# Cross-attention block on one core: gathered q and k rows on other partitions, and another order in the setup

## The chip, the cores and the metric

The kernel runs on one core of one Trainium2 chip. The metric is the device time of one execution in microseconds, lower is better. TensorE (PE), VectorE (DVE), ScalarE (ACT) and GpSimd (POOL) each work through their own list of instructions; SyncE (SP) does little here but issue the transfers (DMAs) between HBM and the on-chip memory SBUF. The lists meet at semaphores only.

## The reference, cut to what matters

```python
B, N, C = 32, 256, 256;  M = 77;  H = 16;  D = 16;  hid = 1024
xq, c = layer_norm(x), layer_norm(context)
q = (xq @ q_w).reshape(B, N, H, D)
k, v = split((c @ kv_w).reshape(B, M, 2, H, D))
attn = einsum('bnhd,bmhd->bhnm', q, k) * D ** -0.5
attn = softmax(where(xa_mask[:, None], -finfo.max, attn), axis=-1)
x = x + einsum('bhnm,bmhd->bnhd', attn, v).reshape(B, N, C) @ proj_w + proj_b
x = x + gelu(layer_norm(x) @ fc1_w + fc1_b) @ fc2_w + fc2_b
```

## The kernel before, in words

The 32 batches are worked in 16 pairs (512 tokens, `TN`, a pair). Every engine runs `body(j, par, mlp, prep, ahead)` once a pair; bodies 0 and 1 are written out, a hardware loop runs 2 to 13, then two more are written out. Inside body j the scores, exponentials and output projection of pair j are interleaved on PE with the second MLP layer of pair j-1 and with the preparation of pair j+1: transposes of its normalised context (`cT`) and x (`xT`), `k_proj`, `q_proj`, `v_proj`, and `maxima`. Body 0 has no MLP work of an earlier pair. Where PE would stand still in the setup, `keep_warm` multiplies weights into an unused bank; nobody reads the result. Nothing but the order in which these lists are written decides what runs when.

Precise products are made of three single-pass products of high and low parts (`product`). The scores need q and k of every head side by side on the contraction rows, so q and k are stored to HBM (`qd`, `kd`: `store_q`, `store_k`) and read back as gathers of 16-row pieces into three matrices: `QR` and `KR` for a first, rough product whose row maxima (DVE, `row_max`) give the softmax shift, `QM` and `KM` for the exact scores. The contraction of `QM` is 127 rows: rows 0 to 76 hold the mask (copied by ACT or POOL from `mask_u8`, times a fixed pattern in `KM`), rows 77 to 124 hold the 16 dimensions times three terms of q, rows 125 and 126 the shift (`spread_shift`). `QR` is built alike on 125 rows, with three heads side by side on rows 77 to 124.

The setup before body 0: weights are loaded and split, pair 0 is projected, its q and k go through HBM, its twelve banks of maxima are multiplied on PE (`maxima(0, r)`) and reduced on DVE (`first_row_max`), the shifts of batch 0 and then of batch 1 are transposed (`first_shift_transpose`) and spread. Then body 0 starts with `cT(1)`, `xT(1)`, 13 `keep_warm` and `scores(0, 0)`.

Names and lines that the steps below touch, by the numbers of the profile: L1096 the rough product, L893 its reduction in the setup and L791 in the bodies, L1126 scores, L620 exp, L1200 `keep_warm`, L1042 every precise product (q, k, v, output projection `PROJ`, fc1), L1151 the transposes `hT` of the second layer norm, which wait for eight reduced banks of the next pair, L269/L270 the gather into KR, L341/L343 (L347/L349 in the setup) into QR, L276 into KM, L354/L360 into QM, L280 and L284 the stores of k and q, L294 and L288 the spread of the shift, L314 the load of `xin` (x again, for the residual), L507 POOL's `add_proj_b`, L518 POOL's `low_o`, L524 POOL's low parts of fc2's weights.

Three orders matter. POOL in body 0: `mask_rows_for_maxima(1)`, `add_proj_b(0)` (waits for `xin`), `low_o(0, 0)`, `low_o(0, 1)`. The projection of batch b waits for `low_o`, and DVE's transpose of batch 1's attention output waits for `low_o(0, 0)`, since both use the tile `oT`. SP in body 0: context and x of pair 2, store k, store half of q, gather KR, store the other half of q, gather QR (waits until q has landed in HBM), gather KM and QM.

Of the kernel before, what the change touches and what calls it, by code (L numbers as in the profile page):

```python
# [9 lines left out]
def xattn_block(nc, x, ctx, maskT, vec_columns, q_w, kv_w, proj_rows, proj_b, fc1_w, fc2_w, fc2_b, out):  # L10
# [30 lines left out]
    RROWS = QROWS + M  # L41
    RBANKS = TT * RG // 2
# [6 lines left out]
    with es:  # L49
# [28 lines left out]
        mask_u8 = sb("mask_u8", [M, NB, N], maskT.dtype)  # L78
# [32 lines left out]
        with ExitStack() as before_g:  # L111
# [4 lines left out]
            pat_m, pat_r = raw("pat_m", 1, MX), raw("pat_r", 1, MX)  # L116
# [22 lines left out]
        def max_bank(r):  # L139

            return RB[r % 4] if r < 8 else ST[r % 2]

# [92 lines left out]
        QM_LOADS, QR_LOADS, K_STORES, Q_STORES = 6 * 16, 6 * 16, 2 * 16, 4 * 16  # L235
# [26 lines left out]

        def gather_k_for_maxima(eng, j):
            if not isinstance(j, int) or j > 0:
                eng.wait_ge(k_stored, k_stores(j + 1))
            for_max = KR[M:RROWS].bitcast(F32).rearrange("p h b m -> p h (b m)")
            per_head = kd[0].rearrange("(h d) n -> d h n", d=D)
            for a in range(3):
                eng.dma_start(for_max[a * D:(a + 1) * D, a:H - 1:3], per_head[:, a:H - 1:3]).then_inc(qr_loaded, 16)  # L269
            eng.dma_start(for_max[2 * D:, H - 1:H], per_head[:, H - 1:H]).then_inc(qr_loaded, 16)  # L270
# [29 lines left out]
        def _(sp):  # L300
# [38 lines left out]
            def gather_q_for_maxima(j):  # L339
                sp.wait_ge(q_stored, q_stores(j + 1))  # L340
                sp.dma_start(QR[M:RROWS, 0:RG - 1].bitcast(F32),  # L341
                             qd[0, 0:(RG - 1) * QROWS].rearrange("(g r) n -> r g n", r=QROWS)).then_inc(qr_loaded, 16)
                sp.dma_start(QR[M:RROWS, RG - 1].bitcast(F32), qd[0, H * D - QROWS:]).then_inc(qr_loaded, 16)  # L343

            def first_q_for_maxima(b, done):
                toks = slice(b * N, (b + 1) * N)
                sp.dma_start(QR[M:RROWS, 0:RG - 1, toks].bitcast(F32),  # L347
                             qd[0, 0:(RG - 1) * QROWS, toks].rearrange("(g r) n -> r g n", r=QROWS)).then_inc(done, 16)
                sp.dma_start(QR[M:RROWS, RG - 1, toks].bitcast(F32), qd[0, H * D - QROWS:, toks]).then_inc(done, 16)  # L349

            def first_q_for_scores(b, rows, done):
                toks = slice(b * N, (b + 1) * N)
                for a in rows:
                    sp.dma_start(QM[M + a:SHIFT:3, :, toks].bitcast(F32),  # L354
                                 qd[(0, 1, 0)[a], :, toks].rearrange("(h d) n -> d h n", d=D)).then_inc(done, 16)

            def gather_q_for_scores(j):
                sp.wait_ge(s_mm, PB * j)
                for a, part in enumerate((0, 1, 0)):
                    sp.dma_start(QM[M + a:SHIFT:3].bitcast(F32),  # L360
                                 qd[part].rearrange("(h d) n -> d h n", d=D)).then_inc(qm_loaded, 16)
# [27 lines left out]
            sp.wait_ge(first_q_stored, G * 16)  # L389
            first_q_for_maxima(0, qr_loaded)  # L390
            first_q_for_maxima(1, qr_late)
            sp.wait_ge(pat_done, 2)
            gather_k_for_scores(sp, 0, (0, 1))
            first_q_for_scores(0, (0, 2), qm_loaded)
# [4 lines left out]
            spread_first_shift(sp, 0)  # L399
            first_q_for_scores(1, (0, 1, 2), qm_late)  # L400
            spread_first_shift(sp, 1)
            load_mask(1)
            load_xin(0, 0)

            def body(j, par, mlp, prep, ahead):
# [3 lines left out]
                if prep:  # L409
                    store_k(j + 1)  # L410
# [25 lines left out]
        def _(pool):  # L436
# [4 lines left out]
            pool.memset(pat_m[:], 0.0).then_inc(patterns, 1)  # L441
            pool.memset(pat_r[:], 0.0).then_inc(patterns, 1)
# [3 lines left out]
            pool.wait_ge(patterns, 2)  # L446
# [965 lines left out]
```

## Time and profile before

| | us |
|---|---|
| median of 3 runs | 783.61 (782.18 to 784.01) |
| the profiled execution, device time | 780.9 |
| its span in the trace | 779.0 |
| its mean granted TensorE clock | 0.993 |

The page gives busy times of the engines, the span in 40 slices, the chain of waits that ended last and the costliest groups of instructions. A wait is listed with the engine that stood still, the line of its next instruction and what released it. A gap on PE before body 1 is worth reading, since the later bodies repeat.

### The profile page before, as it was taken

The page shows a single profiled execution, that of the slowest core. Times are in us where ns is not written, and L with a number is a line of the kernel's source. Part 1 is how long each engine was busy: PE and PEld are TensorE (multiplying, and loading weights), DVE is VectorE, ACT ScalarE, POOL GpSimd, SP SyncE. Part 2 cuts the span into 40 slices and gives each one's busy share as a digit, 9 for nine tenths or more (in the row PEclk, how much of TensorE's full clock was granted, in tenths as well). Part 3 has the DMA queues.
Part 4 walks back from the last instruction along what each step waited for, and adds up shares of the span by engine and source line. Part 5 has one row for each costly group of instructions (what it writes and reads, how often), then busy time and mean ns, then how long its engine had stood idle before and what let it go on. Part 6 is the DMA issues. An engine that isn't in the chain of part 4 may idle for free.

```text
span 779.0 us, 17095 instructions
## 1 busy us (share of the span) xinstructions
PE 755.7 (97%) x5647; PEld 636.6 (82%) x5647; DVE 600.8 (77%) x1376; ACT 525.2 (67%) x776; POOL 225.4 (29%) x217
## 2 busy tenths in 40 slices
PE   8796999999999999999999999999999999999998
PEld 7665788797988879798887979888797988879687
DVE  6777778788887888788787888878787888867453
ACT  5755776767677676767767676776767677676732
POOL 3153240423324042332404233240423324041230
PEclk9899999999999999999999999999999999999999
DMA  7999486694948759494875949487594948649100
GB/s 254 173 170 135 93 157 110 156 125 124 140 114 160 113 151 127 130 135 109 161 113 151 127 132 135 107 161 113 152 127 133 137 104 162 112 115 130 32 28 28
DMA packets 90869, 99.93 MB, mean 128 GB/s; under 512 B 8854, under 2 KB 66166, under 8 KB 90838
## 3 DMA queue, kind: packets, MB, share of 16 engines
q1 hardware_dynamic: 90134, 98.83, 68.0%
q10 hardware_dynamic: 704, 0.69, 0.3%
q8 instruction: 18, 0.29, 0.2%
q14 instruction: 13, 0.11, 0.1%
HBM read 68.18 MB, written 30.28 MB: 126 GB/s over the span
## 4 chain that ended last, share of the span: by engine, by line
PE 81%; DMA 7%; DVE 3%; ACT 3%; issue 3%; SPq 1%; ACTq 0%; POOL 0%; DVEq 0%; POOLq 0%
PE A L1042 25%; PE F L1042 14%; PE ST L1126 8%; PE A L1135 7%; PE F L1180 7%; PE F L1181 6%; PE F L1182 6%; PE ST L1096 3%; DMA QR<-qd 3%; PE A L1151 2%; PE A L1096 1%; DMA kd<-k_lo 1%; ACT probs L620 1%; ACT L714 1%; DMA qd<-q_lo 1%
## 5 line engine op out<-in xcount | busy, mean ns | idle before, releaser
L620 ACT ACTIVATE probs<-ST 78x512 f32<-78x512 f32 x256 | 137.5, 587 | 51.0 <-PE ST L1126 46.8
L1180 PE MATMUL F<-w_hi,g_hi 128*128 128x256 f32 x480 | 138.4, 288 | 0.0
L1181 PE MATMUL F<-w_lo,g_hi 128*128 128x256 f32 x480 | 134.3, 280 | 0.0
L1182 PE MATMUL F<-w_hi,g_lo 128*128 128x256 f32 x480 | 134.2, 280 | 0.0
L720 DVE TENSOR_TENSOR g_lo<-g_f,g_hi 128x512 fp32r<-128x512 f32 x128 | 88.2, 689 | 33.2 <-ACT g_hi L654 30.7
L640 ACT ACTIVATE QM<-mask_u 77x2048 fp32r<-77x2048 uint8 x60 | 111.2, 1901 | 0.0
L1126 PE MATMUL ST<-QM,KM 127*78 127x256 f32 x512 | 94.6, 296 | 4.5 <-ACT probs L620 2.2
L1180 PEld LDWEIGHTS F<-w_hi,g_hi 128*128 128x128 f32 x480 | 90.4, 188 | 6.2 <-issue 6.2
L1126 PEld LDWEIGHTS ST<-QM,KM 127*78 127x78 f32 x512 | 59.0, 146 | 39.0 <-ACT probs L620 30.6
L1181 PEld LDWEIGHTS F<-w_lo,g_hi 128*128 128x128 f32 x480 | 90.7, 189 | 0.0
L1182 PEld LDWEIGHTS F<-w_hi,g_lo 128*128 128x128 f32 x480 | 90.2, 188 | 0.0
L501 POOL TENSOR_TENSOR pool_carrier<-eps 128x1 f32<-128x1 f32 x15 | 2.9, 193 | 274.0 <-DVE g_hi L851 269.1
L518 POOL TENSOR_TENSOR oT_lo<-g_f,oT_hi 128x512 fp32r<-128x512 f32 x32 | 41.6, 1299 | 138.3 <-ACT oT_hi L627 138.3
L645 ACT ACTIVATE xT_hi<-A 128x512 fp32r<-128x512 f32 x32 | 17.4, 595 | 88.8 <-PE A L1151 88.8
L791 DVE TENSOR_REDUCE shift<-ST 128x6 f32<-128x462 f32 (+1 forms) x120 | 63.3, 569 | 16.8 <-PE ST L1096 15.4
L1135 PE MATMUL A<-probs,V 78*32 78x256 f32 x1024 | 68.7, 385 | 0.4 <-ACT probs L620 0.4
L652 ACT ACTIVATE g_f<-F,bias 128x512 f32<-128x512 f32 x64 | 44.1, 689 | 34.0 <-issue 20.1
L808 DVE STREAM_TRANSPOSE o_tok<-A 128x512 f32<-128x512 f32 x64 | 43.1, 693 | 20.3 <-PE A L1135 20.3
L652 ACT ACTIVATE g_f<-A,bias 128x512 f32<-128x512 f32 x64 | 44.1, 689 | 19.6 <-PE A L1042 14.3
L1042 PE MATMUL F<-xT_hi,w_hi 128*128 128x512 f32 x128 | 52.5, 410 | 0.3 <-DVE xT_lo L720 0.3
L1042 PE MATMUL A<-xT_hi,w_hi 128*128 128x512 f32 x128 | 51.8, 405 | 0.0
L720 DVE TENSOR_TENSOR xT_lo<-A,xT_hi 128x512 fp32r<-128x512 f32 x64 | 42.7, 688 | 11.7 <-ACT xT_hi L645 10.7
(188 smaller groups left out, 1916.0 us busy)
## 6 DMA issues: line engine op xcount, KB each, us to landing
QM<-qd SPq DMA_DIRECT2D x45, 512.0 KB, 14.9
xa<-in_x SPq DMA_DIRECT2D x16, 512.0 KB, 4.0
qd<-q_hi SPq DMA_DIRECT2D x32, 256.0 KB, 2.1
xin<-in_x SPq DMA_DIRECT2D x16, 512.0 KB, 5.6
qd<-q_lo SPq DMA_DIRECT2D x30, 256.0 KB, 2.0
out<-xin SPq DMA_DIRECT2D x30, 256.0 KB, 7.6
KM<-kd SPq DMA_DIRECT2D x48, 156.0 KB, 6.9
QR<-qd SPq DMA_DIRECT2D x15, 480.0 KB, 5.4
```

The source lines that it names most:

```text
L620: act.activation(probs[:, quad % NSLOT, 2 * (p % 2):2 * (p % 2) + 2], ST[p % 2][0:MX].rearrange("p (h n) -> p h n", n=N), ACT.Exp, scale=S ...
L640: act.activation(QM[0:M, heads], mask_u8[:].rearrange("p b n -> p (b n)").unsqueeze(1).to_broadcast([M, H // MASK_PARTS, TN]), ACT.Copy).t ...
L652: act.activation(g_f[k % 2][:], FC1[k % 4][:], ACT.Gelu, bias=b1).then_inc(gelu_done, 1)
L720: return dve.tensor_tensor(dst, src, hi.bitcast(F32), ALU.subtract)
L791: dve.tensor_reduce(shift[:, 6 * c:6 * c + n, t], max_bank(r)[:, 0:n * MX].rearrange("p (h m) -> p h m", m=MX)[:, :, 0:M], X, ALU.max).the ...
L808: dve.transpose(o_tok[:, qq].rearrange("p n e -> p (n e)"), A[2 * b + qq][:]).then_inc(o_tok_done, 1)
L1042: last = pe.matmul(dst, a, b, start=(n == 0), stop=(n == 3 * len(terms) - 1))
L1126: last = pe.matmul(ST[p % 2][0:MX, i * N:(i + 1) * N], KM[:, h, b], QM[:, h, b * N:(b + 1) * N], start=True, stop=True)
L1135: last = pe.matmul(A[2 * b + qq][32 * i:32 * (i + 1), g * N:(g + 1) * N], V[:, b, 4 * q + i], probs[:, quad % NSLOT, i], start=True, stop= ...
L1180: pe.matmul(dst, g_hi[:, k, tok], w2_hi[:, k], start=(k == 0), stop=False)
L1181: pe.matmul(dst, g_hi[:, k, tok], w2_lo[:, k], start=False, stop=False)
L1182: last = pe.matmul(dst, g_lo[:, k, tok], w2_hi[:, k], start=False, stop=(k == HC - 1))
```

## The change

1. **Rows.** The three terms of head dimension d now stand on rows 7d, 7d+1, 7d+2 (`term_rows`, step 7) and the 77 keys' mask on the rows between and behind them, in `QM`, `KM`, `QR` and `KR`. The mask is laid out on 125 rows ahead of the launch, with zeros on the rows of the terms, and copied whole; so the gathers of q must now wait for the mask copy (`mask_max`, `mask_qk`). The gathers into KR and QR are three DMAs each, of 16 rows (before: four for KR; for QR two, of 48 rows). The gather into QM is cut in two halves of the heads, six DMAs, each half behind two of ACT's four mask copies. The pattern is one tile, `pat`, with seven instructions of POOL that select instead of four.
2. **Setup, PE.** `first_maxima` takes the place of `maxima(0, r)` with more PSUM banks (`FIRST_RB`). `cT(1)` and `xT(1)` run behind the eighth of the twelve banks; banks 10 and 11 run behind `scores(0, 1)`. The 13 `keep_warm` ahead of the scores and 8 others are gone. In body 0 `k_proj(1)` runs ahead of `scores(0, 2)`, `q_proj(1, 0)` ahead of `scores(0, 4)` and `q_proj(1, 1)` ahead of the first `attend`.
3. **Setup, DVE and ACT.** `normalise_x(1)` runs ahead of the second half of the reductions; the MLP's weight parts are spread between k_low and q_low of pair 1. ACT makes `QM`'s mask of batch 0 in gaps of the first 16 us, and k_high and q_high of pair 1 behind the exponentials 1, 3 and 5 (before: 3, 5 and 9).
4. **Loads.** `load_xin(0)` moves from the end of the setup to behind the gather of QR(1) in body 0.

On PE, from the eighth bank on to the second pair of scores (`A<-pw_hi`, the projection, comes later); before:

```order
L1096 MATMUL A<-KR,QR 128x234 x2
L1205 MATMUL A<-ident,shift 64x128
L1200 MATMUL A<-kvw_hi 128x512
L1096 MATMUL ST<-KR,QR 128x234
...
L1205 MATMUL A<-ident,shift 64x128
L1200 MATMUL A<-kvw_hi 128x512 x4
L1050 MATMUL A<-ident,cn 128x77 x4
L1056 MATMUL A<-ident,xa 128x128 x8
L1200 MATMUL F<-kvw_hi 128x512 x13
L1126 MATMUL ST<-QM,KM 78x256 x8
```

and after:

```order
L1252 MATMUL F<-KR,QR 128x234 x2
L1258 MATMUL A<-ident,shift 64x128
L1083 MATMUL A<-ident,cn 128x77 x4
L1089 MATMUL A<-ident,xa 128x128 x8
L1252 MATMUL F<-KR,QR 128x234
...
L1157 MATMUL ST<-QM,KM 78x256 x4
L1252 MATMUL F<-KR,QR 128x234 x3
L1252 MATMUL F<-KR,QR 128x78
L1258 MATMUL A<-ident,shift 64x128
L1075 MATMUL A<-cT_hi,kvw_hi 128x156
```

The transposes of pair 1 moved ahead of the last four banks, the weight multiplications between them left, and the products of k (`A<-cT_hi,kvw_hi`) start behind four of the score products, where eight stood before.

On SP, from the last spread of the setup on into body 0; before:

```order
L294 DMA QM<-o_tok 2x16x128 x2
L327 DMA mask_u<-in_mask_BxSxS_bk 77x2x256
L314 DMA xin<-in_x 128x4x256
L320 DMA cn<-in_ctx 77x2x256
L308 DMA xa<-in_x 128x4x256
L280 DMA kd<-k_hi 128x2x156
...
L284 DMA qd<-q_lo 128x512
L341 DMA QR<-qd 48x5x512
L343 DMA QR<-qd 48x512
L276 DMA KM<-kd 16x16x156 x3
L360 DMA QM<-qd 16x16x512 x3
L327 DMA mask_u<-in_mask_BxSxS_bk 77x2x256
```

and after:

```order
L305 DMA QM<-o_tok 2x16x128
L338 DMA mask_u<-in_mask_BxSxS_bk 125x2x256
L331 DMA cn<-in_ctx 77x2x256
L319 DMA xa<-in_x 128x4x256
...
L295 DMA qd<-q_lo 128x512
L355 DMA QR<-qd 16x6x512
L355 DMA QR<-qd 16x5x512 x2
L325 DMA xin<-in_x 128x4x256
L287 DMA KM<-kd 16x16x156
```

The load of xin now stands behind two stores' round trips and the gather into QR.

The core of the diff:

```diff
+        FIRST_RB = (ST[0], ST[1], A[0], A[3], ST[0], ST[1], A[0], F[1], F[0], A[0], F[1], F[0])
+        def term_rows(a):
+            return slice(a, a + STEP * (D - 1) + 1, STEP)
-                eng.dma_start(KM[M + a:SHIFT:3].bitcast(F32).rearrange("p h b m -> p h (b m)"),
+                eng.dma_start(KM[term_rows(a)].bitcast(F32).rearrange("p h b m -> p h (b m)"),
...
             def gather_q_for_maxima(j):
                 sp.wait_ge(q_stored, q_stores(j + 1))
-                sp.dma_start(QR[M:RROWS, 0:RG - 1].bitcast(F32),
-                             qd[0, 0:(RG - 1) * QROWS].rearrange("(g r) n -> r g n", r=QROWS)).then_inc(qr_loaded, 16)
-                sp.dma_start(QR[M:RROWS, RG - 1].bitcast(F32), qd[0, H * D - QROWS:]).then_inc(qr_loaded, 16)
+                sp.wait_ge(mask_max, j + 1)
+                per_head = qd[0].rearrange("(h d) n -> d h n", d=D)
+                for a in range(3):
+                    sp.dma_start(QR[term_rows(a), 0:(H - a + 2) // 3].bitcast(F32), per_head[:, a:H:3]).then_inc(qr_loaded, 16)
...
-            def gather_q_for_scores(j):
-                sp.wait_ge(s_mm, PB * j)
+            def gather_q_for_scores(j, half):
+                sp.wait_ge(mask_qk, MASK_PARTS * j + (half + 1) * MASK_PARTS // 2)
+                heads = slice(half * H // 2, (half + 1) * H // 2)
...
@@ sync, end of the setup and body @@
             load_mask(1)
-            load_xin(0, 0)
...
                     gather_q_for_maxima(j + 1)
+                    if not mlp:
+                        load_xin(0, 0)
                     gather_k_for_scores(sp, j + 1)
-                    gather_q_for_scores(j + 1)
+                    gather_q_for_scores(j + 1, 0)
                 if mlp:
                     store(j - 1, 1 - par, 0)
+                if prep:
+                    gather_q_for_scores(j + 1, 1)
@@ vector, end of the setup @@
             normalise_ctx(1)
+            normalise_x(1)
             for r in range(RBANKS // 2, RBANKS):
                 first_row_max(r)
             first_shifts(1)
-            normalise_x(1)
-            mlp_weight_low(0)
-            mlp_weight_low(1)
@@ tensor, setup and body @@
+            for r in range(8):
+                first_maxima(r)
+                if 4 <= r < 7:
                     keep_warm(A[2], 1)
-            first_shift_transpose(1)
-            keep_warm(A[2], 4)
+            first_shift_transpose(0)
+            cT(1)
+            pe.wait_ge(first_shiftT_done, 1)
+            xT(1, 1)
+            xT(1, 0)
+            first_maxima(8)
+            first_maxima(9)
...
-                if not mlp:
-                    keep_warm(F[0], 13)
...
+                if not mlp:
+                    first_maxima(10)
+                    first_maxima(11)
+                    first_shift_transpose(1)
+                    k_proj(j + 1)
                 scores(j, 2)
```

## Rows read from the trace of the kernel before

**Rows 1.** The page: busy times, PE and granted clock in 40 slices.
```profile
PE 755.7 (97%) x5647; PEld 636.6 (82%) x5647; DVE 600.8 (77%) x1376; ACT 525.2 (67%) x776; POOL 225.4 (29%) x217
PE   8796999999999999999999999999999999999998
PEclk9899999999999999999999999999999999999999
```

**Rows 2.** Busy time by stretch: stretch, its length, PE, PEld, DVE, ACT, POOL, clock, DMA share, GB/s.
```profile
20.00:40.00 20.00, 15.65 (x100) 13.71 (x99) 14.95 (x42) 13.39 (x20) 3.04 (x3) 0.83 1.03 167
60.00:80.00 20.00, 14.03 (x85) 12.54 (x86) 14.54 (x35) 11.46 (x12) 5.93 (x8) 0.91 1.06 131
400.00:500.00 100.00, 99.64 (x739) 84.06 (x738) 81.47 (x186) 71.60 (x108) 27.03 (x24) 1.00 0.68 127
```

**Rows 3.** PE's waits: who was waited for, us in total, times, longest.
```profile
PE ST L1096 <- DMA QR<-qd: 6.4, 4, 2.9
```

**Rows 4.** PE in order of time: start, us, instruction, idle before it and its releaser.
```profile
29.06 1.20 PE L1096 MATMUL ST<-KR,QR 125*128 125x234 f32 x4 [2.91 <-DMA QR<-qd]
39.77 3.26 PE L1200 MATMUL F<-kvw_hi 128*128 128x512 f32 x13
61.77 0.36 PE L1042 MATMUL A<-pw_hi,oT_hi 128*128 128x256 f32 x1 [1.94 <-POOL oT_lo L518]
65.93 0.72 PE L1096 MATMUL ST<-KR,QR 125*128 125x234 f32 x4 [2.49 <-DMA QR<-qd]
74.66 1.09 PE L1151 MATMUL A<-ident,o_tok 128*128 128x128 f32 x8 [1.71 <-DVE shift L791]
111.54 0.71 PE L1096 MATMUL ST<-KR,QR 125*128 125x234 f32 x4 [0.54 <-DMA QR<-qd]
```

**Rows 5.** Stretches as in rows 2: gathers alone, stores, idle and half-speed PE.
```profile
28.00:42.00 14.00, 11.51 (x59) 9.73 (x60) 11.88 (x28) 6.70 (x11) 3.12 (x2) 0.82 1.18 128
57.00:59.00 2.00, 1.88 (x14) 1.23 (x15) 1.90 (x5) 0.07 (x1) 0.00 (x0) 1.00 0.77 273
59.80:66.00 6.20, 1.77 (x14) 1.57 (x13) 4.71 (x11) 5.27 (x5) 3.48 (x4) 1.00 0.93 137
67.60:71.10 3.50, 3.50 (x16) 3.16 (x16) 2.52 (x10) 1.44 (x1) 0.49 (x2) 0.55 1.09 133
```

**Rows 6.** DMAs issued at 29.36, 24.52, 48.05, 57.26 and 84.44: KB, us to landing.
```profile
QM<-qd SPq DMA_DIRECT2D x1, 256.0 KB, 12.1
QR<-qd SPq DMA_DIRECT2D x1, 48.0 KB, 4.5
kd<-k_lo SPq DMA_DIRECT2D x1, 156.0 KB, 7.0
qd<-q_lo SPq DMA_DIRECT2D x1, 256.0 KB, 2.3
xin<-in_x SPq DMA_DIRECT2D x1, 512.0 KB, 5.5
```

**Rows 7.** SP's spread of the first shift, and ACT's mask copies, in order of time.
```profile
34.04 1.42 SPq L294 DMA_DIRECT2D QM<-o_tok  x2
...
24.42 3.88 ACT L579 ACTIVATE QM<-mask_u 77x1024 fp32r<-77x1024 uint8 x4
```

**Rows 8.** DVE in order of time.
```profile
40.04 0.48 DVE L754 TENSOR_REDUCE A<-A 128x4 f32<-128x308 f32 x1
44.11 1.45 DVE L866 SCALAR_TENSOR_TENSOR w_lo<-raw_w,columns,w_hi 128x512 fp32r<-128x512 f32 x1
46.93 0.66 DVE L770 SCALAR_TENSOR_TENSOR k_lo<-A,bias,k_hi 128x154 fp32r<-128x154 f32 x2 [1.37 <-ACT k_hi L603]
68.62 0.69 DVE L826 TENSOR_TENSOR xin<-A,xin 128x512 f32<-128x512 f32 x1 [0.91 <-PE A L1042]
```

**Rows 9.** POOL in order of time.
```profile
52.71 2.37 POOL L507 TENSOR_TENSOR xin<-xin,projb 128x1024 f32<-128x1024 f32 x1
60.35 1.27 POOL L518 TENSOR_TENSOR oT_lo<-g_f,oT_hi 128x512 fp32r<-128x512 f32 x1 [5.27 <-ACT oT_hi L627]
```

More of the change, by code:

```diff
@@ L688, in body @@
                     exp(j, p)
[L689 removed]
+                    if not mlp and p == 1:
+                        first_shift_rows(1)
                         k_high(j + 1)
[L691 removed]
+                    if mlp and prep and p == 3:
+                        k_high(j + 1)
+                    if not mlp and p == 3:
                         q_high(j + 1, 0)
[L693 removed]
+                    if mlp and prep and p == 5:
+                        q_high(j + 1, 0)
+                    if not mlp and p == 5:
+                        q_high(j + 1, 1)
+                    if mlp and prep and p == 9:
                         q_high(j + 1, 1)
@@ L980, in body @@
                     ln_moments(j + 2)
-                if prep:
+                if mlp and prep:
                     q_low(j + 1, 1)
@@ L1200, in keep_warm, with first_maxima @@
                     pe.matmul(bank[:], kvw_hi[:, 0, 0:P], kvw_hi[:, 0], start=True, stop=True)
+            def first_maxima(r):
+                t, c = divmod(r, RG // 2)
+                tok = slice(t * P, (t + 1) * P)
+                if r == 0:
+                    pe.wait_ge(qr_loaded, QR_LOADS)
+                    pe.wait_ge(mask_max, 1)
+                if r == RBANKS // 2:
+                    pe.wait_ge(qr_late, 3 * 16)
+                if r in (4, 5, 6):
+                    pe.wait_ge(max_done, r - 3)
+                if r == 7:
+                    pe.wait_ge(q_lo_done, G)
+                if r == 8:
+                    pe.wait_ge(setup_done, QKV_READY + 1)
+                if r > 8:
+                    pe.wait_ge(max_done, r - 2)
+                for half in range(2):
+                    h = 6 * c + 3 * half
+                    n = min(3, H - h)
+                    last = pe.matmul(FIRST_RB[r][:, 3 * half * MX:(3 * half + n) * MX].rearrange("p (h m) -> p h m", m=MX),
+                                     QR[:, 2 * c + half, tok], KR[:, h:h + n, t // TB], start=True, stop=True)
+                last.then_inc(r_mm, 1)
             def first_shift_transpose(b):
                 pe.wait_ge((first_shift_done, shift_done)[b], 2)
-                pe.wait_ge(first_shiftT_done, b)
-                pe.transpose(SHT[0:2 * H * TB, b * P:(b + 1) * P], first_shift[:, b].rearrange("p t h -> p (t h)"),
+                pe.transpose(FIRST_SHT[b][0:2 * H * TB, 0:P], first_shift[:, b].rearrange("p t h -> p (t h)"),
                              ident[:]).then_inc((first_shiftT_mm, shiftT_mm)[b], 1)
@@ L1255, in body @@
                 pe.wait_ge(v_done, j + 1)
-                if prep:
+                if mlp and prep:
                     cT(j + 1)
@@ L1286, in body @@
                 scores(j, 7)
-                if prep:
+                if mlp and prep:
                     q_proj(j + 1, 1)
@@ L1395 @@
         'ctx_1024': _np.asarray(inputs['ctx_1024']),
-        'mask_BxSxS2_bk0': _np.asarray(inputs['mask_BxSxS2_bk0']).transpose(0, 2, 1),
+        'mask_BxSxS2_bk0': None,
         'vectors': _np.concatenate([_np.asarray(inputs[n]) for n in _VECTORS]).reshape(-1, 128).T,
     }
+    m = _np.asarray(inputs['mask_BxSxS2_bk0'])
+    key = _np.arange(m.shape[2])
+    rows = _np.where(key < 64, 7 * (key // 4) + 3 + key % 4, key + 48)
+    laid_out['mask_BxSxS2_bk0'] = _np.zeros((m.shape[0], 125, m.shape[1]), m.dtype)
+    laid_out['mask_BxSxS2_bk0'][:, rows] = m.transpose(0, 2, 1)
     for name in _PLAIN:
```

119 lines of the change are left out of this document (65 added, 54 removed).

## The prediction

> **What bounds the kernel now.** I read the 40 slices and the windows first. From the fifth slice on PE is busy nine tenths or more of every slice at the full clock [rows 1], and a stretch in the loop shows 99.64 of 100 us [rows 2]. The reader is to see there that no other engine and no transfer can give anything in the loop, unless PE waits for it. The setup and body 0 are different: 4.35 us of 20 to 40 and 5.97 us of 60 to 80 have no PE work [rows 2]. Then PE's waits: the longest are for the gather into QR, four times, 6.4 us [rows 3]. In order of time they are 2.91 us ahead of the first maxima, 2.49 us ahead of pair 1's, and 0.54 us in body 1; the remaining one is 0.46 us (what is left of the 6.4) in a later body [rows 3, 4]. What looks busy is partly filler: the 13 keep_warm of 3.26 us ahead of the first scores do nothing but pass time [rows 4]. So the span is a chain of setup up to the transposes hT of pair 0, which start at 74.66 [rows 4], and behind it a fixed amount of PE work. I forecast when hT starts after the change, and what the loop gives.
>
> **The loop, part by part.** PE has the same products there. The gathers show 128 GB/s at a DMA share of 1.18, where stores from all partitions show 273 GB/s at 0.77 [rows 5]: the DMA engines are occupied and move little, so something at the gathers' rows holds them up. Those rows are 77 to 124, and the change spreads them over nearly the whole height. I take 1.8 times the rate, between 1 (the rows are not the reason) and 2.1 (273 against 128).
>
> The Trainium skill (SBUF — State Buffer, "Door 1: The DMA port swizzle") says that a transfer's rate follows how many of 16 ports its partitions reach, and that partitions 64 to 127 reach eight of them. By it each old gather reaches eight ports and each new one 14, a rate of 1.75 times; its own 27 GB/s a port would allow 218 GB/s before, and the trace shows 128, so the page's limit is not reached here and the ratio is not certain.
>
> Two waits of together 0.9 to 1.0 us (body 1 and one later body) are what a faster QR gather can take off the loop. The third issue of the QR gather costs 0.45 us of SP, and the rate more than repays it. Gain 0.9; with an unchanged rate a loss of up to 0.5 in each of the 15 gathers, 6 us, less where there is slack. The QM gather now starts behind ACT's mask copies, some 5 to 8 us later; its scores come more than 20 us behind it, so that cover is wide. SP's store of the first half of the output and the next mask load, which stand behind it in SP's list, move by 3 us at most and are waited for 15 us later. Nothing.
>
> **The setup, step by step.** Times are those of the trace before, and in brackets what the step had there.
>
> 1. ACT's two mask copies of 0.97 us each [rows 7] before the weights arrive are free (ACT stands still there); one more of 0.97 us sits ahead of the copy of x's transpose, of which about 0.5 is covered by ACT's idle time. q is 0.3 us later. POOL's three more selections of 0.25 us end before anybody needs its next result.
> 2. First maxima: three issues of 0.45 us instead of two; the second landed 4.5 us after its issue [rows 6]. With the faster rate I take 2.8 us behind the third: 24.5 + 0.9 + 2.8 = 28.2 (29.06, rows 4). Bounds 27.5 to 30.
> 3. Banks 0 to 7 and the first shift transpose: 4.95 us at half clock, as before; ACT's copy 0.3; two spread issues of 0.7 each [rows 7], of which the second lands some 2.2 us after its start (between 2.0, the fastest small transfers of the trace, and 3): 28.2 + 4.95 + 0.3 + 0.75 + 2.2 = 36.4. PE meanwhile does cT(1), xT(1) and banks 8 and 9, which are ready at about 36. The gather into QM was the real limit before: the last of it was issued at 29.36 and landed 12.1 us later, at 41.5 [rows 6]. At 1.8 times the rate it lands near 35. So the first scores start at 36.6 (43.02, behind the 13 keep_warm).
> 4. Banks 10 and 11 behind them, DVE's two reductions and the shifts: +2.3, to 38.9. Then DVE splits cT and xT of pair 1, 4.07 us as from 40.04 to 44.11 [rows 8], one weight part of 0.7 and k_low 0.6: k_lo is ready at 44.3 (47.55). The old weight part took 1.45 us [rows 8], while POOL was on its own weight parts; POOL now has them behind it.
> 5. Store of k: the second DMA took 7.0 us [rows 6] because x, xin and QM were in flight; now they aren't, and I take 2.6 as in later bodies: 44.3 + 0.4 + 2.6 = 47.3 (55.0).
> 6. KR gather 1.3, q stores 0.9 of issue, of which the last lands after 2.3 [rows 6]: 51.4 (59.6), and 1.25 for QR's three issues: 52.6. **QR lands near 55.5 and is no longer waited for.**
> 7. What is late next: the load of xin. It had its place at 40.07 and a lot of slack; now it is issued at 52.6. Alone it took 5.5 us [rows 6]; I take 4.6, since no other writer competes but QR. It lands at 57.2, POOL adds the bias in 2.37 and makes low_o in 1.27 [rows 9]: 60.9. **The projection of batch 0 starts at 60.9 (61.77, rows 4).** PE's eight keep_warm end at 57.1, so PE stands still for 3.8 us.
> 8. Batch 1: DVE's transpose 0.7, ACT's copy 0.6, POOL's low_o 1.3: 63.6 for the projection. At full clock it is over at 65.1, DVE is free from 65.4, and adds the projection of batch 1 to x at 65.4 (68.62, rows 8). From there to hT DVE is busy without a gap for 6.0 us in both. Gain 3.2.
>
> **The clock.** The trace shows PE at a granted clock of 1.00 while it does 1.77 us in 6.2, and then 0.55, near the lower of its two levels (1.2 against 2.4 GHz), over 3.5 us of full work [rows 5]. PE's pause of step 7 is as long as those. At half speed the two projections and the maxima between them (3.6 us) last up to 3.6 us more, of which the first projection's and half of the second's are on the path: I take 1.5, between 0 and 2. The sparse work between 33 and 42 costs something too, but DVE's splits run beside it: 0.3, between 0 and 1.3.
>
> Sum: 3.2 - 1.5 - 0.3 + 0.9 = 2.3 us. 780.9 - 2.3 = 778.6 as a profiled execution. The median of the runs shown is 2.7 us above the profiled one; I keep that distance: 783.6 - 2.3 = **781.3**.
>
> **Rivals.**
> - *The load of xin doesn't bind, or binds less.* If it lands with QR, 1 to 2 us earlier, and the clock stays up, projections start at 59.5 and the gain is 3.2 + 1.4 + 0.9 = 5.5: 778.1. For it: POOL waits for nothing else, and the unforced chain (q stored at 51.4) would allow 56. Against it: two round trips through HBM stand ahead of the load in SP's list, and each of my terms for them is already near the shortest of the trace.
> - *Moved slack eats the gain.* Half clock from 37 to 44 makes the products of k and q 1.3 to 1.4 us longer each, q_lo is ready at 50.5 instead of 48, and xin, two round trips later, pushes the projections to 63.5: gain 3.2 - 2.6 - 1.5 + 0.9 = 0, 783.6.
> - *Slower.* The rows are not what holds the gathers up, and they stay at 128 GB/s. Then QM of batch 0 lands at 42, the first scores start there, banks 10 and 11, the splits and k_lo follow at 49.7, and xin is issued at 58 and lands at 63; the projection starts at 66.7 against 61.77. That is 5 us more, partly won back since the waits on DVE shrink by 2.2, and the QR waits in the loop stay or grow: 787.5. It decides once the gathers' rate is under about 1.2 times the old one. For it: packets that were written to neighbouring rows might wait for something other than the row, such as the read side, which doesn't change. Against it: the same buffers in HBM are written, and x is read, at twice the rate.
>
> **How the numbers follow.** Forecast, xin as the new limit with gain 1.2 to 3.6: 0.47. Less bound: 0.20. Gain eaten: 0.23. Slower: 0.10. A measurement of this kernel tells 0.3%, 2.35 us, from no change. The forecast's own range (780.0 to 782.4) lies across that bound, half on each side, so faster takes 0.24 + 0.20 and some of the rest: 0.46, same 0.44, slower 0.10. The range for 8 in 10 takes in the first two rivals and their spread: 778.0 to 784.6. It leaves out the slow gathers, and a gain above 5.6.
>
> **What the profile after would show.** Step 2: QM and QR gathers well above 128 GB/s at a share under 1.1. Step 3: no wait of the first scores behind 38. Steps 5 and 6: QR's wait of 2.49 us gone and those of the loop too. Step 7: POOL's L507 group waits for the DMA of xin, and a wait of PE for POOL's oT_lo of 3 to 5 us instead of 1.94. Clock: a half-speed stretch that begins between 58 and 64. I'm wrong if the DMA rate in the gathers is as before, if PE waits in the loop for the mask or QM, or if PE's wait for oT_lo is released by ACT's copy rather than by the bias on POOL.

## The result: slower, where faster or no change was forecast

| | before | after |
|---|---|---|
| median of 6 runs, us | 783.56 (782.18 to 784.01) | 786.9 (784.94 to 789.42) |
| ratio to before, 95% interval | | 1.006 (1.0037 to 1.0084) |
| the profiled execution, device time | 780.9 | 784.94 |
| its span / its mean granted clock | 779.0 / 0.993 | 783.2 / 0.983 |

The time lies above the range on record (778.0 to 784.6) and on the other side of no change. The page of after, for [rows 1]:

```profile
PE   8886999999999999999999999999999999999998
...
PEclk9888999999999999999999999999999999999999
```

From the fifth slice on PE and its clock read as before. The changed kernel's stretches, for [rows 2] and [rows 5], with the columns of [rows 2]:

```profile
20.00:40.00 20.00, 17.43 (x104) 15.10 (x102) 14.28 (x42) 12.07 (x19) 5.76 (x6) 0.83 0.78 215
42.00:46.00 4.00, 3.32 (x16) 3.32 (x17) 3.83 (x7) 0.43 (x2) 0.00 (x0) 0.50 0.23 62
60.00:80.00 20.00, 12.34 (x62) 10.53 (x61) 10.70 (x28) 7.40 (x6) 8.22 (x9) 0.79 0.53 137
400.00:500.00 100.00, 99.61 (x736) 84.05 (x735) 81.77 (x188) 70.97 (x107) 27.04 (x24) 1.00 0.41 121
```

The loop moves the same data at a DMA share of 0.41 instead of 0.68, and PE is as full as before. The loss lies at 60 to 80: 12.34 us of PE work instead of 14.03, at a granted clock of 0.79 instead of 0.91. PE in order of time, for [rows 4]:

```profile
29.47 1.20 PE L1252 MATMUL ST<-KR,QR 125*128 125x234 f32 x4
38.81 0.67 PE L1157 MATMUL ST<-QM,KM 127*78 127x256 f32 x4 [1.47 <-DMA QM<-o_tok]
41.26 0.42 PE L1258 MATMUL A<-ident,shift 128*64 128x128 f32 x1 [1.40 <-DVE shift L934]
42.68 0.50 PE L1075 MATMUL A<-cT_hi,kvw_hi 128*128 128x156 f32 x1 [1.00 <-DVE cT_lo L751]
...
66.70 0.55 PE L1075 MATMUL A<-pw_hi,oT_hi 128*128 128x256 f32 x1 [5.19 <-POOL oT_lo L541]
78.58 1.97 PE L1182 MATMUL A<-ident,o_tok 128*128 128x128 f32 x8 [1.85 <-DVE shift L822]
```

Three things are to be seen. The first scores start at 38.81, where they started at 42.86 in the kernel before, right behind the 13 keep_warm of [rows 4]. Twenty-eight microseconds later that lead of 4 us is a lag of 4.9: the projection of batch 0 starts at 66.70 instead of 61.77, behind a wait of 5.19 us for POOL's `oT_lo`. And the transposes hT start 3.92 us later (78.58 against 74.66) and take 1.97 us, against 1.09. The span is 4.2 us longer: 3.9 from hT's start, 0.9 from hT's own half-speed start, and -0.6 from everything behind it, in which two waits for QR of together 1.0 us are gone and a little more half-speed work has come.

What released POOL is in its own list, and what released that, in SP's. POOL's and then SP's rows of after, in order of time:

```profile
46.36 2.75 POOL L525 CAST QR<-mask_u 125x3072 fp32r<-125x3072 uint8 x1
62.99 2.34 POOL L530 TENSOR_TENSOR xin<-xin,projb 128x1024 f32<-128x1024 f32 x1 [13.88 <-DMA xin<-in_x]
65.29 1.26 POOL L541 TENSOR_TENSOR oT_lo<-g_f,oT_hi 128x512 fp32r<-128x512 f32 x1
```

```profile
44.40 0.40 SPq L319 DMA_DIRECT2D xa<-in_x  x1
...
47.46 0.47 SPq L291 DMA_DIRECT2D kd<-k_lo  x1
...
51.71 1.91 SPq L280 DMA_DIRECT2D KR<-kd  x3
...
54.28 0.43 SPq L295 DMA_DIRECT2D qd<-q_lo  x1
56.65 1.85 SPq L355 DMA_DIRECT2D QR<-qd  x3
58.55 0.59 SPq L325 DMA_DIRECT2D xin<-in_x  x1
```

POOL stands still for 13.88 us for the load of `xin`. SP issues that load at 58.55, since the gather into KR waits until k has landed in HBM (51.7) and the gather into QR until q has (56.6). The last rows of after are the DMAs: KB and us from issue to landing. The first three are medians of the whole run (in before, the same gather into KM took 6.9 us and the store of the output 7.6), the next two are of 42 to 64 us.

```profile
QM<-qd SPq DMA_DIRECT2D x96, 256.0 KB, 4.0
KM<-kd SPq DMA_DIRECT2D x48, 156.0 KB, 3.0
out<-xin SPq DMA_DIRECT2D x30, 256.0 KB, 3.1
...
kd<-k_lo SPq DMA_DIRECT2D x1, 156.0 KB, 4.2
xin<-in_x SPq DMA_DIRECT2D x1, 512.0 KB, 4.4
```

The share of the queue that carries them fell from 68.0 to 42.4% at 98 MB in both:

```profile
q1 hardware_dynamic: 90134, 98.83, 68.0%
```

```profile
q1 hardware_dynamic: 91766, 98.18, 42.4%
```

(before first, after second). So the rows did what was claimed for them: the share fell by a factor of 1.6 (the forecast took 1.8 for the rate), and the landing times by more. The rest of the change ate it.

### The profile page after: what moved, and what is told of

Read it like the earlier page. It is cut to its first block, busy times and chain, and to the rows that moved or that the text cites. A ratio compares the mean times of both kernels' runs of the same rounds, so it can differ in the third digit from the quotient of the medians.

```text
span 783.2 us, 17155 instructions
## 1 busy us (share of the span) xinstructions
PE 758.2 (97%) x5626; PEld 639.1 (82%) x5626; DVE 602.0 (77%) x1376; ACT 526.0 (67%) x776; POOL 225.4 (29%) x219
## 3 DMA queue, kind: packets, MB, share of 16 engines
q1 hardware_dynamic: 91766, 98.18, 42.4%
## 4 chain that ended last, share of the span: by engine, by line
PE 87%; issue 5%; ACT 3%; DMA 2%; DVE 2%; POOL 1%; SPq 0%; ACTq 0%; DVEq 0%; POOLq 0%
PE A L1075 26%; PE F L1075 14%; PE ST L1157 9%; PE A L1166 8%; PE F L1211 7%; PE F L1212 6%; PE F L1213 6%; PE ST L1127 3%; PE A L1182 2%; PE A L1127 1%; ACT L745 1%; ACT probs L643 1%; DMA raw_q<-in_L_xattn_q_w 1%; PE F L1220 0%; PE A L1264 0%
## 5 line engine op out<-in xcount | busy, mean ns | idle before, releaser
L663 ACT ACTIVATE QM<-mask_u 125x2048 fp32r<-125x2048 uint8 x60 | 111.3, 1902 | 0.0
L822 DVE TENSOR_REDUCE shift<-ST 128x6 f32<-128x462 f32 (+1 forms) x120 | 63.4, 571 | 16.1 <-PE ST L1127 14.9
L530 POOL TENSOR_TENSOR xin<-xin,projb 128x1024 f32<-128x1024 f32 x16 | 38.1, 2380 | 60.4 <-DVE g_lo L751 46.6
```

Of the source, the lines that this page charges most:

```text
L663: act.activation(QM[0:RROWS, heads], mask_u8[:].rearrange("p b n -> p (b n)").unsqueeze(1).to_broadcast([RROWS, H // MASK_PARTS, TN]), ACT ...
L822: dve.tensor_reduce(shift[:, 6 * c:6 * c + n, t], max_bank(r)[:, 0:n * MX].rearrange("p (h m) -> p h m", m=MX)[:, :, 0:M], X, ALU.max).the ...
```

## Experiments

The kernel before ran beside every group of kernels; its medians there were 782.1, 782.8 and 782.2 us. Three theories had to be told apart:

- **X**: the load of `xin` in its new place costs what was lost. Its rival: the new order or the rows do, and `xin` only shows the wait.
- **M**: the mask is now loaded with 125 rows, and this holds up the loads of the weights behind it. Its rival: the spread of `raw_q`'s landing is chance.
- **O**: the new order of the setup is worth its 4 us of earlier scores. Its rival: the 13 keep_warm were time that the chain behind needs anyway.

### X taken out and put in alone

The changed kernel with `xin` loaded where it was before (a_xin_early), and the kernel before with `xin` moved (b_xin_late). Line numbers are left out.

```diff
             load_mask(1)
+            load_xin(0, 0)
...
-                    if not mlp:
-                        load_xin(0, 0)
                     gather_k_for_scores(sp, j + 1)
```

> The changed kernel with one thing undone: the load of xin(0) stands at the end of the setup again, behind the mask load. Theory X (the late load of xin is the new bound): POOL no longer waits 13.88 us for it, low_o of batch 0 follows ACT's copy at about 59.3 instead of 65.3, the projection starts near 60.6 instead of 66.7, hT near 72 instead of 78.6, and the median falls by 6 to 7 us, to 780 to 781. Theory C (PE's sparse work lets the clock fall, and that is the loss): PE's pause before the projection shrinks but the half-speed stretches from 39 to 46 stay; at most 2 us, 785. Theory F (the first 20 us got slower): no change, 787.

> The kernel before with one thing changed: the load of xin(0) behind the gather of QR(1) in body 0. Theory X: it is issued at about 60.4 and lands at 65 to 66 (QR and KM are in flight), POOL's bias and low_o take 3.6 us, the projection starts near 69.5 instead of 61.8, and the time grows by 6 to 8 us, to 790 to 791. Theories C and F: the late load is hidden and the time stays within 2 us of 783.6.

Measured: a_xin_early 779.2 us, ratio 0.9963 (0.9943 to 0.9983), a little below what theory X expected; b_xin_late 789.28 us, ratio 1.0074 (1.0047 to 1.0101), a little below too. POOL and PE in a_xin_early, then in b_xin_late:

```profile
49.01 2.83 POOL L529 TENSOR_TENSOR xin<-xin,projb 128x1024 f32<-128x1024 f32 x1
...
60.07 1.31 POOL L540 TENSOR_TENSOR oT_lo<-g_f,oT_hi 128x512 fp32r<-128x512 f32 x1 [8.23 <-ACT oT_hi L649]
```

```profile
61.53 0.36 PE L1074 MATMUL A<-pw_hi,oT_hi 128*128 128x256 f32 x1 [0.26 <-POOL oT_lo L540]
```

```profile
66.95 2.34 POOL L508 TENSOR_TENSOR xin<-xin,projb 128x1024 f32<-128x1024 f32 x1 [13.10 <-DMA xin<-in_x]
```

```profile
70.65 0.55 PE L1043 MATMUL A<-pw_hi,oT_hi 128*128 128x256 f32 x1 [9.69 <-POOL oT_lo L519]
```

With the load in its old place the bias is added at 49.01, as a job of POOL's idle time, and PE waits 0.26 us instead of 5.19. The same edit costs 5.8 us in the kernel before (0.0074 of 782.1) and 7.6 in the changed one (1.006 less 0.9963, of 782). X is shown from both sides.

### The rows alone, and the mask on 128 rows

rows_only is the kernel before with part 1 of the change (the diff ahead of the prediction, from `term_rows` to the gathers) and nothing else. rows_mask128 is the same with the mask laid out and loaded on 128 rows, of which 125 are used; a_mask128 is the changed kernel with that one edit.

```diff
-        mask_u8 = sb("mask_u8", [RROWS, NB, N], maskT.dtype)
+        mask_u8 = sb("mask_u8", [P, NB, N], maskT.dtype)
...
-    laid_out['mask_BxSxS2_bk0'] = _np.zeros((m.shape[0], 125, m.shape[1]), m.dtype)
+    laid_out['mask_BxSxS2_bk0'] = _np.zeros((m.shape[0], 128, m.shape[1]), m.dtype)
```

> The kernel before with the new rows (gathers, mask on 125 rows, pattern, the waits that they need) and nothing of the new order; xin is loaded early as before. If the rows make the gathers faster and that is all: maxima of pair 1 wait 2 us less at 65.9, the QR waits in the loop go (1 us), the 13 keep_warm still stand ahead of the first scores: 1 to 4 us faster, 780 to 782.5. Theory F (the front is slower because of the mask's 125 rows): the weights for q land 1.2 us later as in the changed kernel, and the first gather into QR starts near 25.5 instead of 24.2: the gain shrinks to 0 to 2 us.

> The kernel before with the new rows alone (as rows_only), and the mask laid out on 128 rows instead of 125, which changes nothing but its load. Theory M (a load of 125 rows is carried by few DMA engines and holds up the weights queued behind it): the weights for q land at 8.6 to 8.9 instead of 9.9 to 10.2, the first banks of maxima start 1.3 us earlier, and the median falls by about 1.3 us against rows_only, to a ratio near 0.991 of the kernel before. Theory N (the late weights come from more bytes, 62.5 against 38.5 KB, or by chance): 64 KB land as late, no change against 0.993.

> The changed kernel with the mask laid out on 128 rows. Theory M: the weights for q land at 8.7 instead of 9.95, everything up to the load of xin moves 1.3 us forward, and the median falls by 1.3 to 2 us: ratio 1.002 to 1.003 against 1.004 to 1.008. Theory N: no change, 1.005.

Measured: rows_only 777.89, ratio 0.9928 (0.9905 to 0.9951), faster than both ranges expected of it; rows_mask128 776.7, 0.9914 (0.9893 to 0.9935); a_mask128 784.03, 1.0009 (0.999 to 1.0028), against 1.006 without the edit.

When PE gets `raw_q`, in before, after, rows_only and a_mask128, in this order:

```profile
8.85 1.02 PE L1189 MATMUL ST<-columns,raw_q 128*128 128x1 f32 x8 [1.00 <-DMA raw_q<-in_L_xattn_q_w]
```

```profile
10.09 1.02 PE L1220 MATMUL ST<-columns,raw_q 128*128 128x1 f32 x8 [1.91 <-DMA raw_q<-in_L_xattn_q_w]
```

```profile
10.18 1.02 PE L1208 MATMUL ST<-columns,raw_q 128*128 128x1 f32 x8 [2.84 <-DMA raw_q<-in_L_xattn_q_w]
```

```profile
8.76 1.02 PE L1220 MATMUL ST<-columns,raw_q 128*128 128x1 f32 x8 [0.60 <-DMA raw_q<-in_L_xattn_q_w]
```

In the five profiles with the mask on 125 rows (after, rows_only, a_xin_early, a_warm28, a_dve) it is 9.6 to 10.2; in the others, where the mask has 77 or 128 rows, 8.6 to 9.1. This much of M is shown: about 1.1 us in the mean. The bytes are not the reason, since 128 rows are more of them. A rule bears on it: the Trainium skill (DMA: Bandwidth & Descriptors, "Why a DMA increments its semaphore by 16 and not by 1") says that such a transfer is spread over the largest number of DMA engines up to 16 that divides the slowest dimension of both its sides. By it 125 rows go to 5 engines, 128 to all 16 and 77 to 11. The traces agree in direction; no row here shows which engine carried what.

The late weight may have a sequel. Of the stretch from 12 to 18 us, before, after and rows_only in this order:

```profile
12.00:18.00 6.00, 5.58 (x36) 4.89 (x35) 5.96 (x11) 3.39 (x7) 0.00 (x0) 1.00 0.78 250
```

```profile
12.00:18.00 6.00, 6.00 (x31) 5.28 (x31) 4.61 (x12) 4.76 (x7) 0.00 (x0) 0.72 0.36 111
```

```profile
12.00:18.00 6.00, 6.00 (x22) 5.07 (x23) 2.98 (x8) 2.34 (x4) 0.00 (x0) 0.50 0.36 111
```

After PE has waited 1.9 or 2.8 us for the weight, it works the transposes and the projection of pair 0 at a granted clock of 0.72 and 0.50, near the lower level (1.2 GHz); after 1.0 us (before), at 1.00. In rows_only the first maxima come at 32.86 instead of 29.06, and still the kernel is faster than before. The length of that wait does not decide it, though: a_dve waited 1.42 us there and was granted 1.00, a_warm28 waited 1.10 and was granted 0.50, and best1, with 128 rows and no such wait, 0.84. What decides the clock there stays open. So does the size of M. In the changed kernel the edit took the ratio from 1.006 to 1.0009, some 4 us, but its one profile, of one of the longest of its runs (786.65), shows no gain (784.8 of span against 783.2: the first maxima come at 28.11, and the projection, which waits for `xin`, at 67.24). In the kernel with the rows alone it took 0.0014, within the intervals, and with `xin` early it shows nothing either: 0.9963 in a_xin_early, 0.9955 in best1 below, which has this edit and another.

### The clock, by more keep_warm

a_warm28 is the changed kernel with 28 `keep_warm` in PE's pause ahead of the projection of batch 0, where the changed kernel and the kernel before have 8.

```diff
-                    keep_warm(F[0], 8)
+                    keep_warm(F[0], 28)
```

> The changed kernel with 28 instead of 8 keep_warm in PE's pause before the projection of batch 0 (20 more are about 4.7 us at full clock, inside the wait of 5.2 us). Theory C: the clock stays at 1.00 from 62 on, the projections, the transposes hT and v_proj run at full speed, and 2 to 3.5 us are won, 783.5 to 785. Theory X alone: the projection still starts at 66.7, DVE's reductions set hT, and only what ran at half clock behind hT (1.4 us) comes back: 785.5.

Measured: 785.52, ratio 1.0032 (1.0014 to 1.005). PE, and the stretch from 60 to 80 us, which had a clock of 0.79 in after:

```profile
70.74 0.36 PE L1075 MATMUL A<-pw_hi,oT_hi 128*128 128x256 f32 x1 [0.36 <-POOL oT_lo L541]
...
81.53 1.09 PE L1182 MATMUL A<-ident,o_tok 128*128 128x128 f32 x8 [1.85 <-DVE shift L822]
```

```profile
60.00:80.00 20.00, 17.53 (x116) 12.73 (x114) 12.56 (x31) 10.61 (x11) 8.30 (x9) 1.00 0.49 139
```

With the pause filled, the clock stays at 1.00, and from the start of the projection to the end of hT it takes 11.9 us, where after took 13.9 (66.70 to 80.55). That is the low end of what theory C expected. The span of this execution doesn't show it (784.7 against 783.2), because its front, which the edit doesn't touch, was late: the first maxima come at 32.70, with the clock at 0.50 from 12 to 18. The medians differ by as much, but the intervals of 1.0032 and 1.006 meet. So the clock's part is seen in one profile each, and its size in the median, some 2 us, isn't settled.

### DVE's weight parts

The forecast had 0.7 us for the weight part ahead of k_low, which took 0.74, and no term for the one between k_low and q_low. That one took 2.80 in after, beside POOL's mask cast of 2.75 (above, at 46.36). DVE of after, in order of time:

```profile
46.27 0.66 DVE L801 SCALAR_TENSOR_TENSOR k_lo<-A,bias,k_hi 128x154 fp32r<-128x154 f32 x2 [0.34 <-ACT k_hi L626]
46.85 2.80 DVE L897 SCALAR_TENSOR_TENSOR w_lo<-raw_w,columns,w_hi 128x512 fp32r<-128x512 f32 x1
...
50.24 0.74 DVE L897 SCALAR_TENSOR_TENSOR w_lo<-raw_w,columns,w_hi 128x512 fp32r<-128x512 f32 x1
```

The same instruction took 0.74 three microseconds later. The part that waits ends just behind POOL's cast (at 49.65; the cast at 49.11). The Trainium skill (SBUF — State Buffer, "Who interferes with whom") says that a VectorE instruction with two inputs in SBUF contends with a GpSimd instruction that reads SBUF, and that this is an exclusive lock; the rows agree. The two k_low, which ran while the cast had begun and read a bank of PSUM, weren't held up (0.66 for both). a_dve moves two parts behind q_low:

```diff
-                    if not mlp:
-                        mlp_weight_low(1)
                     q_low(j + 1, 0)
                 if not mlp:
-                    mlp_weight_low(2)
                     q_low(j + 1, 1)
+                    mlp_weight_low(1)
+                    mlp_weight_low(2)
                     mlp_weight_low(3)
```

> The changed kernel with DVE's weight parts 1 and 2 of the MLP behind both low parts of q in body 0. Theory P (DVE's weight part with two inputs in SBUF stands still while POOL copies the mask, 2.80 us against 0.74): the low part of q's first half starts near 47.5 instead of 49.6, the gather into KR, both stores and the load of xin come 1.5 to 2 us earlier, and the median falls by as much: ratio about 1.003. The weight part is then free to be long where nobody waits. Rival: q_high on ACT (48.4 to 49.1) and q_proj on PE set q's low part, so at most 0.5 us is won.

Measured: 786.16, ratio 1.0045 (1.0028 to 1.0062), no different from the changed kernel. Its DVE:

```profile
48.68 0.75 DVE L807 SCALAR_TENSOR_TENSOR q_lo<-A,bias,q_hi 128x512 fp32r<-128x512 f32 x1 [2.47 <-ACT q_hi L632]
```

DVE now waits 2.47 us for ACT's q_high, which itself waits 1.49 us for PE's products of q. And SP's next step, the gather into KR, waits for k's store to land (51.7 in after), not for q_lo. The 2.80 were real, large, and off the path.

### The order alone

order_only is the changed kernel without part 1 and with `xin` in its old place: parts 2 and 3 on the old rows. At the gathers:

```diff
-                eng.dma_start(KM[term_rows(a)].bitcast(F32).rearrange("p h b m -> p h (b m)"),
+                eng.dma_start(KM[M + a:SHIFT:3].bitcast(F32).rearrange("p h b m -> p h (b m)"),
```

> The kernel before with the new order of PE, DVE and ACT in the setup and body 0, the rows as before, xin loaded early. If the gathers at 128 GB/s set the first scores, as I read the trace of before: they start near 41.5 to 43 as before, k and q of pair 1 follow DVE's splits behind them, k_lo is ready near 49 instead of 47.6, and the time is 0 to 3 us above the kernel before (783 to 786). If the order is good by itself: 780 or less.

Measured: 785.56, ratio 1.0036 (1.0018 to 1.0053). PE of order_only:

```profile
42.24 1.11 PE L1139 MATMUL ST<-QM,KM 127*78 127x256 f32 x4 [5.50 <-DMA QM<-o_tok]
```

With the old rows the scores wait 5.50 us for DMAs: the six gathers into QM ahead of them land after 8.7 us in the median, and the 13 `keep_warm` had lain in that wait. The order needs the rows; the next group asks whether it is worth anything with them.

### All mended, in both orders

best1 is the changed kernel with three edits shown above: `xin` early, the mask on 128 rows, the weight parts behind q_low. best1_warm has 28 keep_warm besides, in the place of a_warm28's, ahead of the projection of batch 0. (What was expected of it speaks of a place ahead of the first maxima; no run changed the `keep_warm` there, so its question on the first 20 us was not put.) rows_mask128_5 is rows_mask128 once more.

> The changed kernel with its three faults mended together: xin loaded at the end of the setup again, the mask on 128 rows, and the MLP's weight parts 1 and 2 behind q_low(1, 1) on DVE. Theory (the faults cost 7 us, 1.2 us and about 0.5 us, and are independent; the new order of the setup then gives nothing over the old one): hT of pair 0 starts at 71 to 72.5, the time is 776 to 778, a ratio to the kernel before of 0.991 to 0.995, no better than the rows alone with the mask on 128 rows (776.7 of 782.8, 0.991). Rival (the new order is worth its 4 us of earlier scores once nothing behind it waits): hT at 69 or earlier, 772 to 774, a ratio of 0.986 to 0.989.

> The same three mended, with 28 products of keep_warm ahead of the first maxima where the changed kernel has 8 (the kernel before has 28). If the half clock of the first 20 us is what the new order pays with, the first maxima and scores run at the full clock and hT starts 1 us sooner: a ratio 0.001 to 0.003 under that of the version with 8. If the products only occupy PE where a transpose or a weight is waiting for it, they push the first maxima from 28.5 to over 31, as they did at 32.7 with the 125-row mask, and nothing is won: a ratio equal or 0.001 to 0.003 above.

> The old order with the new rows and the mask on 128 rows, the fastest so far, once more beside the two versions in the new order, in five rounds, so that the order can be compared on one chip. A repeat should give 0.991 of the kernel before, within 0.002. If the new order with its faults mended is worth something, that version stands at least 0.002 below this one; if not, within 0.002 or above.

Measured: best1 779.93, ratio 0.9955 (0.9933 to 0.9977); best1_warm 783.75, 1.0008 (0.999 to 1.0025); rows_mask128_5 775.55, 0.991 (0.988 to 0.9941). The fastest kernel of the study is the old order with the new rows, twice: 0.9914 and 0.991. Both kernels with the new order are slower than it, and best1 misses the range I had given it. The intervals of 0.9955 and 0.991 just overlap, but ten of best1's twelve runs took longer than five of the other's six. The same comparison with the mask on 125 rows, a_xin_early against rows_only, gives 0.9963 and 0.9928. PE and the stretch from 40 to 50 us, of rows_mask128_5 and then of best1:

```profile
41.88 0.64 PE L1145 MATMUL ST<-QM,KM 127*78 127x256 f32 x4
42.97 0.94 PE L1145 MATMUL ST<-QM,KM 127*78 127x256 f32 x4 [0.45 <-ACT probs L639]
...
69.55 1.09 PE L1170 MATMUL A<-ident,o_tok 128*128 128x128 f32 x8 [1.84 <-DVE shift L810]
```

```profile
40.00:50.00 10.00, 9.53 (x66) 7.18 (x66) 8.52 (x15) 5.55 (x11) 9.35 (x7) 1.00 0.89 240
```

```profile
38.78 0.67 PE L1155 MATMUL ST<-QM,KM 127*78 127x256 f32 x4 [1.25 <-DMA QM<-o_tok]
...
41.23 0.42 PE L1256 MATMUL A<-ident,shift 128*64 128x128 f32 x1 [1.40 <-DVE shift L933]
42.65 0.50 PE L1073 MATMUL A<-cT_hi,kvw_hi 128*128 128x156 f32 x1 [1.00 <-DVE cT_lo L750]
...
45.29 1.06 PE L1155 MATMUL ST<-QM,KM 127*78 127x256 f32 x4
...
73.01 1.97 PE L1180 MATMUL A<-ident,o_tok 128*128 128x128 f32 x8 [1.85 <-DVE shift L821]
```

```profile
40.00:50.00 10.00, 7.77 (x32) 6.78 (x33) 7.03 (x15) 3.62 (x9) 5.47 (x4) 0.66 0.63 182
```

Here is where the lead goes. The new order starts the scores 3.1 us earlier, by leaving out 3.26 us of `keep_warm`. But PE waits 1.25 us ahead of them, for the shift of batch 0, and 1.40 and 1.00 us behind them, for DVE, which has the shift of batch 1 and the splits of pair 1 to do: 3.65 us, about the same time in another place. And only the first four score products have the lead. The next four stand behind these waits and behind the products of k, and start at 45.29 where the old order starts them at 42.97; ACT has no scores to work on meanwhile (it waits 3.58 us there). The projection of batch 0 then starts at 61.74, against 58.68 in the old order. After these waits PE's clock is 0.50 (42 to 46 us in after, above, and in best1), while in the old order it stays at 1.00, and the products of k, 0.28 us each there, take 0.42. The chain that counts, k into HBM, gains nothing: k_lo starts at 46.24 in best1 and at 45.96 in rows_mask128_5.

The granted clock also goes with how the runs of one kernel spread. Of the runs that were timed, each with its own mean granted clock:

| kernel | lowest and highest time, us, with its clock | runs |
|---|---|---|
| before (beside the last group) | 779.78 at 0.995; 787.59 at 0.987 | 23 |
| rows_mask128_5 | 773.52 at 0.996; 779.13 at 0.987 | 6 |
| best1 | 774.78 at 0.993; 782.35 at 0.982 | 12 |
| best1_warm | 781.39 at 0.987; 785.92 at 0.984 | 12 |
| after | 784.94 at 0.983; 789.42 at 0.976 | 6 |

The one run of best1 at 0.993 is as fast as the rows alone at 0.996 and 0.991 (774.5 and 776.1), and at 0.987 three runs of best1 took 778.6 to 780.1 beside 779.1. At an equal clock the two orders are worth about the same, and the new one is granted the lower clock in most of its executions. That is what the records show together; it doesn't say what is cause and what is effect, since a pause of PE costs time and can cost clock at once. No run filled the pauses between 38 and 43 us. a_warm28 filled a pause of 5.2 us further on, and that kept the clock up there. best1_warm put the same products where best1 has no pause: the projection moves from 61.74 to 66.06, hT from 73.01 to 76.61, and the ratio from 0.9955 to 1.0008. How best to fill those gaps stays open.

## Why the prediction was wrong, step by step

The bound was forecast rightly: `xin` is what binds, POOL waits for it, PE waits for `oT_lo` (forecast 3 to 5 us, 5.19 measured), a half-speed stretch begins there, and the waits for QR are gone. What failed is the path up to the issue of `xin`, steps 2 to 7: every term of it was too short, 6.0 us together. The largest miss is step 5, the store of k, where the lag grows by 1.8 us; next is the setup up to the first maxima, 1.3 us. So the term "Gain 3.2" of the sum was a loss of 3.8 (add_x of batch 1 at 72.41 instead of 68.62). With it fell the idea that earlier scores make everything behind them earlier: k_lo was to be ready at 44.3 and was ready at 46.9, where the rows in the old order have it at 46.6. The forecast said: projection at 60.9. It is at 66.70, and the terms add up like this:

| step | forecast | measured | lag so far |
|---|---|---|---|
| 2, first maxima | 28.2 | 29.47 | 1.3 |
| 3, first scores | 36.6 | 38.81 | 2.2 |
| 4, k_lo ready | 44.3 | 46.9 | 2.6 |
| 5, k in HBM | 47.3 | 51.7 | 4.4 |
| 6, q in HBM | 51.4 | 56.6 | 5.2 |
| 7, xin issued | 52.6 | 58.55 | 6.0 |
| 7, xin landed | 57.2 | 63.0 | 5.8 |
| 7, projection of batch 0 | 60.9 | 66.70 | 5.8 |
| 8, add_x of batch 1 | 65.4 | 72.41 | 7.0 |

- **Steps 1 and 2.** I counted ACT's copies of the mask and not its load, though the diff showed it (77 rows became 125). It stands ahead of the weights: 1.2 us. The gather into QR was issued at 25.88 (forecast 24.5), and PE, which had worked at a clock of 0.72 from 12 to 18, was busy up to 29.47 and waited for no gather.
- **Step 3.** The wait that ends last was the spread of the shift, as the forecast had it (36.4, and QM before it). The step was 0.9 us too short.
- **Step 5 failed most.** "Because x, xin and QM were in flight; now they aren't": x still was. SP issues `xa` of pair 2 at 44.40, 512 KB that take 4.1 us, right ahead of the store of k, which took 4.2 instead of 2.6. I had moved `xin` out of the queue in my head, and x with it. That x alone makes the difference isn't shown: in rows_mask128_5 x was in flight as long behind the issue of k_lo (to 48.2, the issue at 47.12), and that store took 3.1.
- **Step 6.** Issues of the gathers. I took some 0.42 us each, as for the gathers of before; the new ones take 0.62 to 0.64 (1.85 for three into QR, 1.91 for three into KR). 1.2 us on the path.
- **Step 7.** The load itself took 4.4 (4.6 forecast), and POOL 2.34 and 1.26: right. The issue was late by all that stood ahead of it.
- **Step 8 and the clock.** 1.5 was taken for the two projections at half speed. The path lost 1.2 there (lag from 5.8 to 7.0), and 0.9 more in hT, for which there was no term; a_warm28, at a clock of 1.00, is 2.0 us shorter over the same work.
- **The loop.** 0.9 forecast, 1.0 of QR waits gone. Right. Its rate was taken as 1.8 times, and the share fell by 1.6 times. The count of eight ports for "each old gather" passed over those into KR, which wrote 16 neighbouring rows each; they are small, and landed after 2.0 us before and 2.2 after.
- **The rival "gathers stay slow"** was the only one that I let end on the slower side, with 0.10, and it did not happen. That the projection came at 66.7, to the tenth the time written down for that rival, is chance: it came there by the forecast's own road, with longer terms. The rival "moved slack eats the gain" had its direction, and 63.5 as its worst. The forecast said of its terms that each was "already near the shortest of the trace", as an argument against the earlier rival; the same words are a warning that the sum of a chain of such terms comes out too short, and the range made no room for that. The distance from 60.9 to no change (61.77) was less than 1 us, while `xin` in its old place had 6.8 us of slack: it landed at 51.2 and was needed at 58.0, which is 60.35 less 2.37. The row of its load in the kernel before, issued at 40.07:

```profile
xin<-in_x SPq DMA_DIRECT2D x1, 512.0 KB, 11.1
```

The 5.5 us of [rows 6], from which the forecast took its "alone", are those of a load issued at 358.10; the one at 84.44 took 5.9.

And what the sum left out:

- **What was missed as a gain.** The rows are worth 0.7 to 0.9% (6 to 7 us) by themselves, where the loop's 0.9 and step 2 to 3 were all that I could name. Nearly all of it is the setup: in rows_mask128_5 the wait for QR of 2.49 us is gone, k and q of pair 1 are in HBM 4 to 5 us earlier (50.2 and 55.3, by the issue of the gathers that wait for them; 55.0 and 59.6 before), and hT starts at 69.55 instead of 74.66, which is 5.1 of 6.3 us of span.

## What to carry to other kernels

A load that is moved behind a store-and-gather round trip starts when the slowest of the steps ahead of it has landed: add these steps with durations from the middle of the trace, and ask what its old place cost (here nothing, and the move cost 6 to 8 us). When one change has a part that relieves a resource and a part that reorders work, time them apart: the rows alone gave -0.9%, the order +0.4%, the move +0.7 to 1.0%. Filler on an engine isn't free time; before it is taken out, look for what the next three instructions behind it will wait for, and before it is put in, whether the engine has a pause there at all.

## What the runs showed of the hardware that I had not expected

- Sixteen-row gathers of the same bytes: from rows 77 to 124, three of 512 KB landed after 14.9 us and the queue had a share of 68.0%; spread over rows 0 to 107, six of 256 KB landed after 4.0 us and the share was 42.4%. The ratio of the shares is 1.6; the landing times shrank by more, since less is queued behind each other. A store of the output that shares the engines went from 7.6 to 3.1 us.
- A load of 63 KB on 125 rows (one of 128 rows does not) delays by about 1.1 us a load of 256 KB behind it (8.6 to 9.1 us became 9.6 to 10.2).
- The clock between the waits: behind pauses of PE of 1.25, 1.40 and 1.00 us, with little work between them, the products of k ran at a granted clock of 0.50, and at 1.00 where 13 filler products stood in that place. A pause of 5.19 us was followed by a stretch at 0.79 in the mean; with 20 more filler products in it, that stretch had 1.00. Executions of one kernel (best1) were granted 0.982 to 0.993 in the mean, and took 782.4 to 774.8 us.
